# Cross-attention: four groups' norms on ScalarE by scale and bias, a root ahead of the capped scores, and the turn of normalised rows one tile later

## The reference

```
x = layernorm(x + self_attention(x))            # 16 heads of 16, no mask
x = layernorm(x + cross_attention(x, ctx) )     # 77 context rows, masked; Wq, Wk, Wv, Wo with biases
x = layernorm(x + experts(x)) * gamma + beta    # 8 experts, 256 -> 512 -> 256, top 2 of 8 by x @ Wg + bg
layernorm(y) = (y - mean) / sqrt(var + 1e-5)    # over the 256 features of a token
```

## Time and profile before

| | us |
|---|---|
| median of 3 runs | 868.59 |
| lowest, highest | 867.88, 879.56 |
| profiled execution, time | 872.9 |
| profiled execution, span | 871.0 |
| TensorE matmul busy | 760.3 (87%) |
| VectorE busy | 643.0 (74%) |
| ScalarE busy | 459.4 (53%) |
| GpSimd busy | 300.6 (35%) |

### The profile page before, as it was taken

The page is one execution under the profiler, slowest core; times in us unless marked ns, Lnnn a source line. Parts: engine busy times, 40 slices in busy tenths (PEclk is TensorE's granted clock), DMA queues, the critical chain, the costliest instruction groups (busy, mean ns, idle before and its releaser), DMA issues.

```text
span 871.0 us, 15027 instructions
## 1 busy us (share of the span) xinstructions
PE 760.3 (87%) x4756; PEld 377.9 (43%) x4756; DVE 643.0 (74%) x1101; ACT 459.4 (53%) x920; POOL 300.6 (35%) x249
## 2 busy tenths in 40 slices
PE   6789999999999899999988977989789999999910
PEld 3442222322222222222213445566578777777700
DVE  3488888887888887787875769889757435688657
ACT  2126677767777676777776633353344444444400
POOL 8000600000000596960002564565802753633321
PEclk9898999999999999999999999999899999999965
DMA  6746040130403599790000450000132322412121
GB/s 196 184 106 158 2 92 19 31 79 1 92 19 75 165 274 276 246 261 15 2 1 1 168 218 1 1 1 19 70 120 61 117 79 72 155 52 75 58 97 48
DMA packets 48515, 80.76 MB, mean 93 GB/s; under 512 B 16116, under 2 KB 35063, under 8 KB 47289
## 3 DMA queue, kind: packets, MB, share of 16 engines
q1 hardware_dynamic: 35017, 45.43, 19.1%
q0 software_dynamic: 9952, 31.29, 11.2%
q10 hardware_dynamic: 3472, 3.08, 1.4%
HBM read 48.21 MB, written 33.11 MB: 93 GB/s over the span
## 4 chain that ended last, share of the span: by engine, by line
PE 59%; DVE 21%; DMA 6%; issue 6%; POOL 4%; ACT 3%; SPq 1%; DVEq 0%; POOLq 0%; ACTq 0%
PE bank L534 12%; PE bank L526 11%; PE quad L507 11%; PE quad L849 8%; DVE rowmax L924 6%; PE bank L863 6%; PE bank L458 2%; ACT probs L1412 2%; POOL x_sorted L1682 2%; DVE sc L1027 1%; PE quad L604 1%; DMA kstack<-k_parts 1%; DVE max L1032 1%; PE bank L636 1%; DMA qstack<-q_parts 1%
## 5 line engine op out<-in xcount | busy, mean ns | idle before, releaser
L924 DVE TENSOR_REDUCE rowmax<-quad 128x1 f32<-128x1024 f32 x256 | 303.1, 1219 | 76.5 <-PE quad L507 75.9
L1412 ACT ACTIVATE probs<-bank 128x512 f32<-128x512 f32 x512 | 284.2, 595 | 116.3 <-PE bank L526 113.4
L526 PE MATMUL bank<-qstack,kstack 98*128 98x512 bf16 x512 | 194.0, 387 | 12.2 <-ACT probs L1412 10.2
L507 PE MATMUL quad<-kstack,qstack 96*128 96x512 bf16 x512 | 178.1, 388 | 15.7 <-DVE rowmax L924 7.4
L534 PE MATMUL bank<-probs,v_all 128*32 128x512 f32 x1024 | 139.1, 611 | 0.0
L526 PEld LDWEIGHTS bank<-qstack,kstack 98*128 98x128 bf16 x512 | 48.9, 97 | 191.4 <-ACT probs L1412 160.2
L849 PE MATMUL quad<-xbT,w_all 128*128 128x128 bf16 x1104 | 100.4, 226 | 8.1 <-issue 4.4
L849 PEld LDWEIGHTS quad<-xbT,w_all 128*128 x1104 | 76.9, 97 | 33.0 <-issue 17.3
L1736 POOL DMA_INDIRECT y_tokens<-ysb,dest x46 | 49.0, 1066 | 97.4 <-DVE ysb L1164 87.4
L507 PEld LDWEIGHTS quad<-kstack,qstack 96*128 96x128 bf16 x512 | 48.6, 99 | 77.4 <-DVE rowmax L924 39.8
L1526 ACT ACTIVATE xbT<-bank 128x512 bf16<-128x512 bf16 x46 | 27.4, 597 | 96.9 <-PE bank L830 96.9
(11 more groups left out here) (173 smaller groups left out, 964.9 us busy)
## 6 DMA issues: line engine op xcount, KB each, us to landing
w_all<-w_split SPq DMA_DIRECT2D x2, 4096.0 KB, 18.0
xb<-x_sorted SPq DMA_DIRECT2D x46, 129.0 KB, 2.1
x_sorted<-blank POOLq DMA_DIRECT2D x6, 774.0 KB, 8.8
w1raw<-in_w POOLq DMA_DIRECT2D x8, 512.0 KB, 5.9
w2raw<-in_w POOLq DMA_DIRECT2D x8, 512.0 KB, 5.6
w_split<-w1two POOLq DMA_DIRECT2D x8, 512.0 KB, 5.1
w_split<-w2two POOLq DMA_DIRECT2D x8, 512.0 KB, 3.5
q_parts<-parts SPq DMA_DIRECT2D x24, 128.0 KB
```

The source lines that it names most:

```text
L507: mm = pe.matmul(bank[2 * (p % 2) + e], q, kstack[slot][0:MAXROW, j, e * 512:e * 512 + 512], start=True, stop=True)
L526: mm = pe.matmul(bank[4 + i % 2], kstack[slot][0:KROWS, j, kt * P:kt * P + P], qstack[slot][0:KROWS, half, j, :], start=True, stop=True)
L924: dve.tensor_reduce(rowmax[:, k % 2, p:p + 1], quad[:, 2 * (p % 2):2 * (p % 2) + 2, :].rearrange("p a n -> p (a n)"), AX_X, ALU.max).then_ ...
L1412: act.activation(probs[:, i % PR, :], bank[4 + i % 2], ACT.Exp, scale=INV4).then_inc(probs_ready, 1)
```

## The change

The norms of x1 for groups 2 and 3, and of x2 for groups 0 and 1, are computed on ScalarE as Identity(scale * x + bias), with scale the reciprocal root and bias the negative product of mean and root, a column that VectorE forms in one more small operation (`scale_rows`). VectorE's norms of the x1 groups 0 and 1 and of the x2 groups 2 and 3 stay. The second batch's root is formed ahead of `take(6)` instead of behind it. TensorE turns x2 between the second and third part of tile 6's and 10's probabilities, where before it did so behind tile 5's and 9's scores; the scores of tiles 9 and 13 (with the logits ahead of them) both come behind the third part. ScalarE copies the turned x2 between those parts, and its bf16 copies of the rows come directly behind the scaling.

```diff
--- before.py
+++ after.py
@@ -234,6 +234,7 @@
         cross_ready, k2_done, v2_done = sem("cross_ready"), sem("k2_done"), sem("v2_done")
         chain, root_wanted, root_done = map(sem, ("chain", "root_wanted", "root_done"))
         last_shifted, last_divided = sem("last_shifted"), sem("last_divided")
+        x1_scaled, x2_scaled = sem("x1_scaled"), sem("x2_scaled")
         x1_done, x1_turned, x1T_done, x1b_done = map(sem, ("x1_done", "x1_turned", "x1T_done", "x1b_done"))
         v2_placed, v2_zeroed = sem("v2_placed"), sem("v2_zeroed")
         q2_ready, q2_done = sem("q2_ready"), sem("q2_done")
@@ -796,12 +797,13 @@
                         next_scores(half)
                 elif i == 3 and g < TG - 1:
                     turn_probs(n, lambda k: None)
+                elif i == 2 and 0 < g < TG - 1:
+                    turn_probs(n, lambda k: turn_x2(g - 1) if k == 0 else next_scores(0))
+                    next_scores(1)
                 else:
                     turn_probs(n, next_scores)
                 if i == 0 and g < TG - 1:
                     turn_x1(g + 1)
-                if i == 1 and 0 < g < TG - 1:
-                    turn_x2(g - 1)
                 if i == 3 and g < TG - 1:
                     values2(g, 0)
                     if n == NT - 5:
@@ -1018,6 +1020,11 @@
                     n = g * 4 + i
                     dve.tensor_scalar(x1[:, i, :], xres[:, n, :], lnv[:, MEAN, n:n + 1], lnv[:, RSTD, n:n + 1],
                                       ALU.subtract, ALU.mult).then_inc(x1_done, 1)
+
+            def scale_rows(lo, hi, done):
+
+                root_moments(lo, hi)
+                dve.scalar_tensor_tensor(lnv[:, 6, lo:hi], lnv[:, MEAN, lo:hi], -1.0, lnv[:, RSTD, lo:hi], ALU.mult, ALU.mult).then_inc(done, 1)
 
             def take(n):
 
@@ -1243,8 +1250,7 @@
                 if i == 1:
                     sum_probs(n + 1)
                     if 0 < g < TG - 1:
-                        root_moments(4 * g - 4, 4 * g)
-                        norm_x2(g - 1)
+                        scale_rows(4 * g - 4, 4 * g, x2_scaled)
                     if g == TG - 1:
                         last_divide(n + 1)
                     sum_probs(n + 2)
@@ -1256,8 +1262,8 @@
                     bn = residual2(g - 1)
                     link(bn)
                     start_moments(4 * g - 4, 4 * g)
-                if i == 3 and g == 1:
-                    norm_x1(3)
+                if n == 3:
+                    scale_rows(KT, NT, x1_scaled)
                 if n == NT - 5:
                     place(0)
                 if n + FAR < NT:
@@ -1270,9 +1276,6 @@
                     bn = add_attention((KT + 6, KT + 7))
                     link(bn)
                     start_moments(KT, NT)
-                elif n == 3:
-                    root_moments(KT, NT)
-                    norm_x1(2)
                 if i == 2 and 0 < g < TG - 1:
                     low_x2(g - 1)
             root_moments(NT - 8, NT - 4)
@@ -1425,6 +1428,8 @@
                 for j, chunks in enumerate(TURNS):
                     if j == 2 and i == 1 and g < TG - 1:
                         keep_q2(g + 1)
+                    if j == 2 and i == 2 and 0 < g < TG - 1:
+                        keep_x2(g - 1)
                     m = 3 * n + j
                     act.wait_ge(p2_turned, m + 1)
                     (half, c), k = chunks[0], len(chunks)
@@ -1432,6 +1437,19 @@
                     dst = pT[0:rows_, half, c:c + k, i * P:i * P + P] if j < 2 else pT[0:rows_, :, c, i * P:i * P + P]
                     act.activation(dst, bank[4 + m % 2][0:rows_, 0:k * P].rearrange("p (k q) -> p k q", q=P), ACT.Copy).then_inc(pT_done, 1)
 
+            def scale_x1(g):
+                act.wait_ge(x1_scaled, 1)
+                act.wait_ge(x1_turned, g * 2)
+                act.wait_ge(x1b_done, 4 * g)
+                for i in range(4):
+                    n = 4 * g + i
+                    act.activation(x1[:, i, :], xres[:, n, :], ACT.Identity, bias=lnv[:, 6, n:n + 1], scale=lnv[:, 2, n:n + 1]).then_inc(x1_done, 1)
+
+            def scale_x2(g):
+                act.wait_ge(x2_scaled, g + 1)
+                for n in range(4 * g, 4 * g + 4):
+                    act.activation(xres[:, n, :], xres[:, n, :], ACT.Identity, bias=lnv[:, 6, n:n + 1], scale=lnv[:, 2, n:n + 1]).then_inc(x2_done, 1)
+
             def keep_x1T(g):
                 for c in range(C2):
                     act.wait_ge(x1_turned, g * 2 + c + 1)
@@ -1461,6 +1479,7 @@
                     act.activation(x2T[:, c, :], bank[X2_BANK[g] + c], ACT.Copy).then_inc(x2T_done, 1)
 
             def keep_high(g):
+                act.wait_ge(x2_done, 4 * g + 4)
                 for n in range(4 * g, 4 * g + 4):
                     act.activation(xrow[:, n, 0:D], xres[:, n, :], ACT.Copy).then_inc(xrow_done, 1)
 
@@ -1512,10 +1531,12 @@
                     break
                 if n + FAR - 1 < NT:
                     exp2(n + FAR - 1)
+                if i == 3 and g < 2:
+                    scale_x1(g + 2)
                 if i == 3:
                     keep_o2(g)
                 if i == 1 and 0 < g < TG - 1:
-                    keep_x2(g - 1)
+                    scale_x2(g - 1)
                     keep_high(g - 1)
 
 
```

## The result

| | us |
|---|---|
| before, median of 20 runs (lowest, highest) | 872.47 (867.13, 879.56) |
| after, median of 20 runs (lowest, highest) | 874.80 (872.21, 879.33) |
| ratio after to before, 95% interval | 1.0040 [1.0021, 1.0059] |
| profiled execution after: time, span | 874.8, 872.9 |

The change makes the kernel slower by 0.4%, some 3.5 us, where a gain of 2.1 us was forecast; the time lies above the range of 864.7 to 870.3. That is far under 2%, but the interval leaves out 1. Part of the miss in the absolute number is the base: the median of before was 868.59 over three runs and is 872.47 over twenty.

What follows compares the result with a forecast made beforehand. The chain to the first expert matmul, through take(13), was taken as the bound. Terms -3.6 + 1.0 + 0 + 0.5 = -2.1 us put the profiled 872.9 at 870.8, hence 866.5 us as median; range 864.7 to 870.3.

Steps and rivals of the forecast that it cites:

- What bounds the kernel: Time gained or lost at take(13), capping tile 13's scores, goes through to the first expert matmul, 48.5 us later.
- C: Group 3's x1 norm leaves VectorE, but take(10) behind it then waits for TensorE's scores: 0.
- A: Tiles 3 and 4, take(6) to take(7): second batch's root and norms leave VectorE, -3.6 us.
- the cover: VectorE's 7.0 us wait ahead of take(6) hides the root moved there; without it, some 3 us.
- The margin of 0.3 us: ScalarE's x1 scalings and first o2 copy end by 521.96, when the second copy began, with 0.3 us spare.
- Rival 3: ScalarE's new wait in front of o2 delays the output projection: A shrinks by 1.1, time 867.6; chance 0.05.
- B: Group 0, root of x2 to take(9): handing work through ScalarE and TensorE takes 9.7 instead of 8.75, +1.0 us.
- D: Group 1, as B, up to take(13): 9.7 instead of 9.18 us, +0.5 us.
- rival 1: TensorE's clock falls in B and D: once 868.2 us, chance 0.27; twice 869.9 us, chance 0.14.
- The price of a fall: Each fall of TensorE's clock loses 1.7 us of full-rate work, costing only where logits and scores lie in it.
- The weighing of gaps: Against rival 1: no single TensorE gap is as long as the 3.99 and 2.8 us before the two earlier falls.
- ring B: Work handed round VectorE, ScalarE and TensorE from group 0's x2 root to capping tile 9; forecast +1.0 us.

Runs made afterwards that it cites:

- the x1 part alone: Changed kernel with x2 norms back on VectorE and the x2 turn back in its place; early root and ScalarE x1 norms stay; ratio to before 0.998.
- the waits filled: Changed kernel plus 12, 6 and 9 unread identity turns in TensorE's waits of tiles 6 and 10; ratio to before 0.9977.
- the kernel before with its waits filled: Kernel before plus unread identity turns on TensorE: 30 ahead of the x1 turn, 8 and 20 ahead of the x2 turns; ratio to before 0.9978.
- both mendings: Changed kernel with x1 scalings behind ScalarE's o2 copies and TensorE's waits of tiles 6 and 10 filled; run twice, ratios to before 0.9930 and 0.9943.
- the x1 part, o2 first and filled: The x1 part alone, with x1 scalings behind the o2 copies and 18 and 20 identity turns ahead of the x2 turns; ratio to before 0.9971.

## Why the prediction was wrong

**What bounds the kernel: right.** Time at take(13) goes through to the experts in every kernel: from take(13) to the first expert matmul it is 48.5 us before, and 48.1 to 48.5 in all thirteen other profiles. take(10) waits for its scores once the x1 norm is gone (2.93 us), and C is 0 within 0.1.

**A: the work right, the cover wrong.** 3.6 us off VectorE were forecast at take(7). 3.8 came in most kernels that have the x1 part. In the changed kernel's profile only 1.0 came. The margin of 0.3 us was read from an execution in which the first half of the values took 6.04 us, its clock being low; with 4.56 us o2 is ready 1.5 us earlier against the same root, and the margin is gone. That alone is still covered by the further us that I had counted (the x1 part alone had its values at 4.56 too, and lost nothing). But where take(5) also comes 1.7 us late, the root does so as well: the scalings start 31.6 us behind the last output copy (515.98 - 484.39) instead of 29.9. Rival 3 named the wait and gave it 0.05; I took the cover as a property of the kernel, where it was one of that execution.

**B and D: the sum right at a held clock, the clock wrong.** Forecast +1.0 and +0.5; with the waits filled the rings are 17.56 and 17.52, that is +1.1 and +0.6 over the kernel before. That D is the cheaper for a low clock in the old ring came out too: the kernel before with its waits filled has 16.45 there, and against it D is +1.1 like B. Even the total is right then: -2.1 forecast, -2.17 measured with both mendings. In the changed kernel they were +4.1 and +4.4. This is the step that failed: the sum put logits and scores in both rings at their full-clock 4.16 us, and with it the fall of the clock at nothing. They took 7.16 us (541.11 to 548.27) and 7.90 (582.69 to 590.59), at a granted clock of 0.50. It is what rival 1 had, the clock falling in both rings, which I gave 0.14 (once: 0.27).

**The price of a fall: wrong by a factor of two.** I took 1.7 us, from the fall of 533 to 539 in the trace of before. By the same sum over the granted clock the falls after took 3.4 us (540 to 548) and 5.1 us (581 to 592) of full-rate work: the clock stayed at 0.50 through 541 to 547 and through 582 to 591, although TensorE worked without a wait from 583 on. Not all of it lay on the path; by comparison with the filled kernel the two cost 3.0 and 3.75 us. Together that is 6.8 where twice 1.7 had been reckoned, and with it and the late o2 the forecast's own sum gives 64.3 + 6.8 + 2.6 = 73.7, against 73.77 measured. Why the clock came back sooner in the trace of before, where TensorE was as busy behind its fall, no run shows.

**The weighing of gaps: wrong.** I held against rival 1 that no single gap was as long as 3.99 or 2.8 us. The longest in ring B after was 1.43, with shorter ones behind it, and the clock fell; so the longest gap alone didn't tell. The row from 541 to 544.5 of before, which I had for the other side, has more work in it (2.38 us of 3.5) than that of 537 to 540 after (1.52 of 3). The Trainium skill, "TensorE: Matmul & The Clock Gate", section "HAM oscillation — how this bites in real kernels", pointed the right way: bursts between waits start cold. The waits of its example are longer than any in the changed kernel's rings, so for gaps this short it is these runs that show it.

**The base.** 868.59 was the median of three runs of a kernel whose twenty runs span 12 us. 3.9 us of the 8.3 between forecast and measured are that. With the right base the forecast would have been 870.4, still 4.4 under the measured time.

**Still open.** What exactly decides when the clock falls and when it comes back. Why the changed kernel's ratio says 3.5 us and its distance 5.5, and why the x1 part, o2 first and filled, gains less than its distance: falls of the clock also come ahead of take(5), in the values, behind tile 13 and at the first experts, in other places in each execution, and one profile each doesn't count them. What they are worth to a ratio isn't known either, so the ratios of the filled kernels can't be laid on the two rings alone. Whether a filling cheaper than turns of the identity holds the clock was not tried.

## What to carry to other kernels

Where an engine's work is cut into pieces by waits on another, look at what it works around its longest operations and at the granted clock there, before and after the change. The longer chain of work on ScalarE cost 1.75 us in the two rings, the clock that fell with it 6.8. A margin read from one execution holds for that execution's clock: ask what it would be with the operation next to it at its full speed. And before crediting a change with what filled waits bring, fill the waits of the old kernel too.

## What the runs showed of the hardware that I had not expected

TensorE's clock fell after waits none of which was over 1.43 us (ring B of the changed kernel). It stayed at the 1.2 GHz level from 582 to 591, with 8.31 of the 9 us busy; in the x1 part alone it did so from 536 to 545 with all 9 busy. 27 turns of the identity, 3.4 us of work in three waits, kept it at 1.00 in ring B (534.0 to 543.6) and made that ring shorter by 3.0 us. Logits, 16 matmuls of eight columns, lose nearly as much by the low clock as wide matmuls do: 3.55 us against 1.92, where eight score matmuls took 4.45 against 2.32.
